# A graph network on one core: the signal of a matmul group stands at a drain of TensorE's queue instead of on its last matmul, in four stages

## The chip, the cores and the metric

One Trainium2 chip, of which the kernel uses one core. The time is device microseconds of one execution. The kernel before was timed in 3 runs: median 5306.26 us, 5303.0 to 5307.47.

## The reference, cut to what matters

6250 nodes with 256 features each, 100000 edges with a source, a destination (edges sorted by destination), three attributes and one of 8 types. Four graph layers one after the other, each on the normalised and rectified nodes and added to them:

```python
h = relu(layernorm(x)); x = x + L0(h, edge_attr, src, dst)        # edge MLP, sum by dst, W2, unit norm
h = relu(layernorm(x)); x = x + L1(h, (src, dst), edge_type)      # x @ W[r] for 8 relations, sum by src
h = relu(layernorm(x)); x = x + L2(h, (src, dst))                 # attention, 8 heads, sum by dst
h = relu(layernorm(x)); x = x + L3(h, (src, dst))                 # normalised sum by src, @ W + b
```

L0 gathers `h[src]` per edge; since its first product is linear up to the bias, the kernel multiplies the nodes first (a table of 6250 x 256, then a gather per edge). L1 likewise needs `h @ W[r]` for all 8 relations: a table of 6250 x 2048. L0's second product is `relu([h, sum] @ W2.T)`, each row divided by its norm.

## The kernel before, in words

The nodes are 49 tiles of 128 rows, the edges 784 columns of 128. The program is a chain of stages; each is a block in which every engine has its own queue and all engines meet at the end. Some stages run many tiles; a `Ring` writes seven tile steps out and repeats them in a loop with the registers of the tile number.

Edges sorted by source are needed too. A record of 8 numbers per edge is written to its place in a list in DRAM by 784 indirect DMAs (`Scatter.run`, L577), one per column of 128 edges, issued by GpSimd. These are spread over the first stages, as work beneath them: `CUTS` (L29) gives each stage its share, counted in rounds of 16 DMAs. GpSimd waits for the DMAs of a half round before it issues the next half of the following round, and a stage can't end before its share has been issued and has landed.

The stages that matter here, in order, with their share of the scatter:

- `list_stage` by source (no scatter yet; the same code as by destination, but with a mask buffer per bucket, so that VectorE runs ahead), `place_stage` (48 DMAs), then the statistics of the nodes (32).
- `table_stage(0)` (64 DMAs): for each tile ScalarE normalises (L2045), TensorE transposes 2 x 128 columns (L2080) and signals `turned`, ScalarE copies (L2050), TensorE multiplies by the weights (L2091) and signals `made`, VectorE adds the bias (L2065), the result goes to DRAM. An fp32 product appears as two matmuls in the trace, so the 256-column product of two halves is four.
- `list_stage` by destination (112 DMAs): 49 times VectorE writes a mask of the edges of one bucket (L404), and TensorE sums it up in two matmuls (L460) and signals `counted`. There are four mask buffers. Then VectorE ranks the counts and the records leave.
- a tile stage and the edge MLP pass (32 and 16 DMAs).
- `sage_update` (160 DMAs), the first update: for each tile TensorE transposes 4 x 128 columns (L2162, `turned`), VectorE copies (L2196), TensorE multiplies (L2168, `made`), ScalarE rectifies and squares (L2143, L2145). After seven tiles VectorE applies the norms and takes the statistics (L2184 to L1912), and only then copies transposes of the next seven.
- `table_stage(1)` (320 DMAs): as layer 0, but 2048 columns, in four blocks of 512 with one `made` each; VectorE copies each block (L2067).

After them come passes over the edges (832, 831, 832 and 586 tiles) in which GpSimd gathers one tile of 128 rows per indirect DMA (L1760, L1591, L675).

TensorE's instructions are issued in the written order: weight load, matmul, and between the groups waits and register arithmetic of the loop. In the kernel before, the last matmul of a group carries the increment of the semaphore (`last.then_inc(...)`).

Of the kernel before, what the change touches and what calls it, by code (L numbers as in the profile page):

```python
# [115 lines left out]
def wait_count(eng, sem, count):  # L116

    if count is not None and not (isinstance(count, int) and count <= 0):
        eng.wait_ge(sem, count)
# [132 lines left out]
def list_stage(nc, c, edges, other=None, first=0, end=0):  # L252
# [10 lines left out]
    with ExitStack() as st:  # L263
# [15 lines left out]
        masked, counted, ranked = sem("masked"), sem("counted"), sem("ranked")  # L279
# [3 lines left out]
        if not by_dst:  # L283
            raw = [sb(f"raw{f}", [TURN, COLS // TURN, P], I32) for f in range(3)]
            real = [r[:, :, :].bitcast(F32) for r in raw]
            turned, kept, key_ready, rest_ready = sem("turned"), sem("kept"), sem("key_ready"), sem("rest_ready")
# [21 lines left out]
        def turned_bank(f, k):  # L308

            return (ps[2 * f + k // 4], k % 4 * TURN + (16 if (f, k // 4) == (2, 1) else 0))  # L310
# [7 lines left out]
        @block.sync  # L318
        def _(sp):
            sp.wait_ge(zeroed, 2)  # L320
            if by_dst:
                load(sp, dst_i, c.dst_in, 1, 0, key_in)
                load(sp, next_i, c.dst_in, 1, 1, rest_in)
            else:
                load_rows(sp, raw[0], c.src_in, key_in)

                full = (sh.NB - 1) * P
                sp.dma_start(c.x[:, 0:sh.NB - 1, :],
                             c.x_in[0:full, :].rearrange("(i p) d -> p i d", p=P)).then_inc(x_in, 16)
                sp.dma_start(c.x[0:sh.LAST, sh.NB - 1, :], c.x_in[full:sh.N, :]).then_inc(x_in, 16)  # L330
                sp.wait_ge(x_in, 32)
            sp.wait_ge(key_in, 48)
            if by_dst:

                sp.wait_ge(recorded, 1)
                sp.dma_start(edges.to.rearrange("(p n) w -> p (n w)", p=P), rec[:, :, :].rearrange("p n w -> p (n w)")).then_inc(written, 16)
                sp.wait_ge(written, 16)
# [103 lines left out]
        @block.tensor  # L441
        def _(pe):
            def turn(f):

                for k in range(COLS // TURN):
                    bank, at = turned_bank(f, k)
                    last = nc.tensor.transpose(bank[:, at:at + TURN], real[f][:, k, :], c.ident[0:TURN, 0:TURN])
                last.then_inc(turned, 1)

            if not by_dst:  # L450
                pe.wait_ge(key_ready, 1)
                turn(0)
            for d in range(NB):
                if not by_dst and d == 8:
                    pe.wait_ge(rest_ready, 2)
                    turn(1)
                    turn(2)
                pe.wait_ge(masked, d + 1)
                for a, z in col_halves:
                    last = nc.tensor.matmul(psT[0:NB, a:z], c.row_of[:, NB - 1 - d:2 * NB - 1 - d], same[:, d % ring, a:z],  # L460
                                            start=(d == 0), stop=(d == NB - 1), skip_group_check=True)
                last.then_inc(counted, 1)
            if by_dst:
                pe.wait_ge(compared, 2)
                nc.tensor.matmul(ps[5][:, 0:1], c.ones[:, :], falls[:, :], start=True, stop=True).then_inc(fallen, 1)
            pe.wait_ge(ranked, 1)
            nc.tensor.matmul(ps[5][0:NB, 8:9], c.before[0:NB, 0:NB], nb[0:NB, 0:1], start=True, stop=True).then_inc(prefixed, 1)
# [807 lines left out]
class Behind:  # L1275
# [16 lines left out]
    def sem(self, name):  # L1292
        return self.nc.alloc_semaphore(f"{name}_behind_{self.nm}")
# [675 lines left out]
def table_stage(nc, c, layer, edges, first, end):  # L1969
# [8 lines left out]
    with ExitStack() as st:  # L1978
# [11 lines left out]
        w_in, hs, turned, hTs, made, outs = [sem(x) for x in ("w_in", "hs", "turned", "hTs", "made", "outs")]  # L1990
# [4 lines left out]
        @block.gpsimd  # L1995
        def _(pool):
            scatter.run(pool)
# [73 lines left out]
        @block.tensor  # L2071
        def _(pe):
            pe.wait_ge(w_in, 16 * {0: 2, 1: NREL}[layer])

            def step(i, u):
                if (t := ring.at(i, u)) is not None:
                    pe.wait_ge(hs, ring.count(t))
                    wait_count(pe, hTs, ring.count(t, 1 if u == 0 else 2))
                    for k in range(2):
                        last = nc.tensor.transpose(psT[u % 2][:, k * P:(k + 1) * P], h[:, u, k * P:(k + 1) * P], c.ident[:, :])  # L2080
                    last.then_inc(turned, 1)
                if (t := ring.at(i, u, 1)) is not None:
                    pe.wait_ge(hTs, ring.count(t))
                    for b, (a, z) in enumerate(blocks):

                        n = NBK * (ring.count(t) - 1) + b
                        back = 4 if NBK * t[1] + b >= 4 else (4 if (NBK * G) % 4 == 0 else (NBK * t[1] + b) + 1)
                        if not (isinstance(n, int) and n - back + 1 <= 0):
                            pe.wait_ge(outs, n - back + 1)
                        for k in range(2):  # L2090
                            last = nc.tensor.matmul(psO[(NBK * t[1] + b) % 4][:, 0:z - a], hT[:, t[1], k * P:(k + 1) * P],  # L2091
                                                    w[:, k, a:z], start=(k == 0), stop=(k == 1))
                        last.then_inc(made, 1)
            ring.run(pe, step, lag=1)


def sage_update(nc, c, edges, first, end):
# [4 lines left out]
    with ExitStack() as st:  # L2102
# [11 lines left out]
        w_in, hns, turned, turned_back, made, rs, sqs, step_, stated = [sem(x) for x in (  # L2114
            "w_in", "hns", "turned", "turned_back", "made", "rs", "sqs", "step_", "stated")]
# [5 lines left out]
        @block.gpsimd  # L2121
        def _(pool):
            scatter.run(pool)
# [29 lines left out]
        @block.tensor  # L2153
        def _(pe):
            pe.wait_ge(w_in, 16)

            def step(i, u):
                if (t := ring.at(i, u)) is not None:
                    pe.wait_ge(hns, ring.count(t))
                    wait_count(pe, turned_back, ring.count(t, 1 if u == 0 else 2))  # L2160
                    for k in range(4):
                        last = nc.tensor.transpose(psT[u % 2][:, k * P:(k + 1) * P], hn[:, u, k * P:(k + 1) * P], c.ident[:, :])  # L2162
                    last.then_inc(turned, 1)
                if (t := ring.at(i, u, 2)) is not None:
                    pe.wait_ge(turned_back, ring.count(t))
                    wait_count(pe, rs, ring.count(t, 1 if t[1] == 0 else 2))
                    for k in range(4):
                        last = nc.tensor.matmul(psO[t[1] % 2][:, 0:D], hnT[:, t[1], k * P:(k + 1) * P], w[:, k, :],  # L2168
                                                start=(k == 0), stop=(k == 3))
                    last.then_inc(made, 1)  # L2170
            ring.run(pe, step, lag=2)

        @block.vector
# [700 lines left out]
```

## Time and profile before

| | kernel before |
|---|---|
| timed, median of 3 | 5306.26 us |
| the profiled execution, first to last instruction | 6597.1 us |
| mean granted clock of TensorE | 0.714 |
| TensorE matmul busy | 3895.4 us (59%) |
| GpSimd busy | 3799.2 us (58%) |
| VectorE busy | 2562.6 us (39%) |
| ScalarE busy | 1792.3 us (27%) |

The profile is of one execution, with every instruction recorded; its span is the 6597.1 us, and a time around that span isn't given. It is a good deal longer than the timed runs, so a duration from it must be set against the timed median with care. Register, branch, semaphore and drain instructions aren't counted as busy. A matmul's end is modelled from its size. "Idle before" is the time an engine stood still, with what ended it; where the engine named had long been done, it was something else.

### The profile page before, as it was taken

The numbers are of one execution on the slowest core, as the hardware profiler recorded it, in microseconds if no ns is written. First come the engines' busy times: TensorE is split into PE (matmuls) and PEld (weight loads), VectorE is DVE, ScalarE is ACT, GpSimd is POOL, SyncE is SP. The second block draws the span as 40 slices with busy tenths as digits, with TensorE's granted clock in tenths as the row PEclk, the third lists the DMA queues.
The fourth block names the chain that finished last, engine by engine and source line by source line (L and its number), as shares of the span: only waits on it lengthen the run. The fifth ranks groups of instructions, "written<-read, shape, count | busy, mean of one in ns | idle before, by whom it ended". The sixth has DMA issues, their size and how long they took to land. (4 is left out here: it accounts for less than half of the span.)

```text
span 6597.1 us, 65618 instructions
## 1 busy us (share of the span) xinstructions
PE 3895.4 (59%) x14913; PEld 2594.0 (39%) x14914; DVE 2562.6 (39%) x8644; ACT 1792.3 (27%) x5648; POOL 3799.2 (58%) x3942
## 2 busy tenths in 40 slices
PE   4232666667641533596455555566777777577777
PEld 2121333333320510242333333355566555455555
DVE  4223444444430300132222222255555555644443
ACT  0111555555530400011000000044444444400000
POOL 3554666666666077402666666666666666277776
PEclk7565666766665765796676666667777777688888
DMA  1011332332310010144433333323333333233332
GB/s 48 20 41 60 88 88 87 89 89 87 88 45 3 0 42 22 59 148 141 124 99 98 98 98 98 96 82 87 87 87 86 87 86 89 77 98 99 99 98 87
DMA packets 277662, 527.83 MB, mean 80 GB/s; under 512 B 80566, under 2 KB 175259, under 8 KB 277049
## 3 DMA queue, kind: packets, MB, share of 16 engines
q0 software_dynamic: 176144, 422.24, 22.5%
q1 hardware_dynamic: 85200, 86.14, 3.9%
q10 hardware_dynamic: 15960, 15.41, 0.7%
q8 instruction: 137, 2.24, 0.1%
q14 instruction: 221, 1.81, 0.1%
HBM read 433.63 MB, written 89.82 MB: 79 GB/s over the span
## 5 line engine op out<-in xcount | busy, mean ns | idle before, releaser
L675 POOL DMA_INDIRECT got_attend_src_dst<-dram_gtab,gather_src x832 | 800.4, 962 | 531.0 <-DVE msg_attend_src_dst L747 320.9
L577 POOL DMA_INDIRECT dram_rec_src<-rec_src x784 | 766.5, 978 | 509.6 <-issue 243.5
L1760 POOL DMA_INDIRECT got_edge_mlp_src_dst<-dram_ptab,gather_src x832 | 786.3, 945 | 463.2 <-DVE pre_edge_mlp_src_dst L1802 252.9
L1591 POOL DMA_INDIRECT got_rgcn<-dram_xtab,gather_of_type x831 | 788.3, 949 | 392.5 <-issue 187.9
L1886 PE MATMUL psS_edge_mlp_src_dst<-msg_edge_mlp_src_dst,hot_edge_mlp_src_dst 128*128 128x256 f32 x1664 | 736.1, 568 | 434.0 <-DVE sage_sums L1783 223.6
L1591 POOL DMA_INDIRECT got_gcn<-dram_htab,gather_rest x586 | 616.5, 1052 | 234.1 <-issue 148.9
L861 PE MATMUL psS_attend_src_dst<-msg_attend_src_dst,hot_attend_src_dst 128*128 128x264 f32 x1664 | 700.8, 513 | 19.5 <-DVE msg_attend_src_dst L747 14.3
L2091 PE MATMUL psO_tab<-w_tab,hT_tab 128*128 128x512 f32 (+1 forms) x980 | 474.4, 633 | 350.1 <-issue 200.5
L1886 PEld LDWEIGHTS psS_edge_mlp_src_dst<-msg_edge_mlp_src_dst,hot_edge_mlp_src_dst 128*128 128x128 f32 x1664 | 388.5, 269 | 589.7 <-issue 338.8
L1682 PE MATMUL psS_rgcn<-got_rgcn,hot_rgcn 128*128 128x257 f32 x1662 | 543.8, 471 | 79.7 <-DMA got_rgcn<-dram_xtab,gather_of_type 55.0
L1783 DVE TENSOR_TENSOR sage_sums<-sage_sums,psS_edge_mlp_src_dst 128x256 f32 x832 | 347.8, 418 | 523.6 <-PE psS_edge_mlp_src_dst L1886 246.1
L884 PE MATMUL psF_attend_src_dst<-ident,hot_attend_src_dst 128*128 128x128 f32 x832 | 314.4, 378 | 356.2 <-ACT hotT_attend_src_dst L832 190.4
L877 PEld LDWEIGHTS psN_attend_src_dst<-node,hotT_attend_src_dst 128*128 128x128 f32 x1664 | 412.5, 253 | 138.1 <-issue 41.4
L1682 PEld LDWEIGHTS psS_rgcn<-got_rgcn,hot_rgcn 128*128 128x128 f32 x1662 | 362.8, 234 | 237.3 <-issue 169.2
L2091 PEld LDWEIGHTS psO_tab<-w_tab,hT_tab 128*128 128x128 f32 x980 | 199.3, 215 | 573.1 <-issue 409.3
L1850 ACT ACTIVATE msg_edge_mlp_src_dst<-pre_edge_mlp_src_dst 128x256 f32<-128x256 f32 x832 | 340.3, 413 | 293.8 <-DVE pre_edge_mlp_src_dst L1802 211.3
L1802 DVE TENSOR_TENSOR pre_edge_mlp_src_dst<-got_edge_mlp_src_dst,psE_edge_mlp_src_dst 128x256 f32<-128x256 f32 x832 | 344.4, 414 | 158.4 <-remote 104.1
L709 DVE TENSOR_TENSOR sums<-sums,psS_attend_src_dst 128x264 f32 x832 | 350.7, 422 | 64.8 <-issue 31.5
L861 PEld LDWEIGHTS psS_attend_src_dst<-msg_attend_src_dst,hot_attend_src_dst 128*128 128x128 f32 x1664 | 361.1, 266 | 37.2 <-DVE msg_attend_src_dst L747 30.7
L1601 DVE TENSOR_SCALAR hot_rgcn<-iota,rel_src 128x128 f32<-128x128 f32 x831 | 216.9, 315 | 390.4 <-remote 180.5
L2067 DVE COPY out_tab<-psO_tab 128x512 f32<-128x512 f32 x196 | 133.7, 690 | 588.4 <-DMA got_edge_mlp_src_dst<-dram_ptab,gather_src 308.9
L1682 PE MATMUL psS_gcn<-got_gcn,hot_gcn 128*128 128x257 f32 x1172 | 322.8, 409 | 64.8 <-issue 30.8
(397 smaller groups left out, 5878.7 us busy)
## 6 DMA issues: line engine op xcount, KB each, us to landing
dram_xtab<-out_tab SPq DMA_DIRECT2D x48, 1024.0 KB
got_edge_mlp_src_dst<-dram_ptab,gather_src POOLq DMA_INDIRECT x832
got_attend_src_dst<-dram_gtab,gather_src POOLq DMA_INDIRECT x832
got_rgcn<-dram_xtab,gather_of_type POOLq DMA_INDIRECT x831
dram_rec_src<-rec_src POOLq DMA_INDIRECT x784
got_gcn<-dram_htab,gather_rest POOLq DMA_INDIRECT x586
dram_gtab<-sums ACTq DMA_DIRECT2D x48, 132.0 KB
x_sb<-x_in SPq DMA_DIRECT2D x1, 6144.0 KB
```

The costliest lines, as they stand in the source:

```text
L577: nc.gpsimd.indirect_dma_start(edges.to, bass.IndirectOffsetOnAxis(edges.rec[:, column, PLACE:PLACE + 1].bitcast(I32), 0), edges.rec[:, co ...
L675: nc.gpsimd.indirect_dma_start(got[:, t % U, 0:w], None, table, bass.IndirectOffsetOnAxis(row_of[:, t:t + 1], 0)).then_inc(row_in[t % U], 16)
L709: nc.vector.tensor_tensor(here, here, psS[t[1] % banks][:, 0:cols], ALU.add).then_inc(added, 1)
L861: nc.tensor.matmul(psS[t[1] % banks][:, 0:cols], hot[:, t[1], :], rows(t), start=True, stop=True).then_inc(sums, 1)
L877: nc.tensor.matmul(psN[t[1] // 2 % 2][:, 2 * HEADS * (t[1] % 2):2 * HEADS * (t[1] % 2 + 1)], hotT[:, t[1] % 4, :], c.node[:, :, :].rearran ...
L1591: nc.gpsimd.indirect_dma_start(got[:, t % U, 0:D], None, table, bass.IndirectOffsetOnAxis(row_of[:, t:t + 1], 0)).then_inc(row_in[t % U], 16)
L1682: nc.tensor.matmul(psS[b % 2][:, 0:D + 1], hot[:, t % U, :], got[:, t % U, 0:D + 1], start=(k == 0), stop=(k == lay.counts[b] - 1), skip_g ...
L1760: nc.gpsimd.indirect_dma_start(got[:, t % U, 0:width], None, table, bass.IndirectOffsetOnAxis(row_of[:, t:t + 1], 0)).then_inc(row_in[t % ...
L1783: nc.vector.tensor_tensor(here, here, psS[t[1] % banks][:, 0:cols], ALU.add).then_inc(added, 1)
L1802: nc.vector.tensor_tensor(pre[:, t[1] % 4, :], got[:, t[1], 0:D], psE[t[1] % 4][:, 0:D], ALU.add).then_inc(pres, 1)
L1886: nc.tensor.matmul(psS[t[1] % banks][:, 0:cols], hot[:, t[1], :], msg[:, t[1] % 8, :], start=True, stop=True).then_inc(sums, 1)
L2091: last = nc.tensor.matmul(psO[(NBK * t[1] + b) % 4][:, 0:z - a], hT[:, t[1], k * P:(k + 1) * P], w[:, k, a:z], start=(k == 0), stop=(k == 1))
```

## The change

In the list stage (by source and by destination: both run the same line), in both table stages and in the first update, the increment no longer stands on the last matmul or transpose of a group. A `drain` of TensorE's queue follows the group and carries it. There are five places in the code; they make 49 signals in each of the two list stages, 49 + 49 in the first table stage, 49 + 196 in the second and 49 + 49 in the update. All other stages keep the increment on the matmul.

```diff
--- before.py
+++ after.py
@@ -459,7 +459,7 @@
                 for a, z in col_halves:
                     last = nc.tensor.matmul(psT[0:NB, a:z], c.row_of[:, NB - 1 - d:2 * NB - 1 - d], same[:, d % ring, a:z],
                                             start=(d == 0), stop=(d == NB - 1), skip_group_check=True)
-                last.then_inc(counted, 1)
+                nc.tensor.drain().then_inc(counted, 1)
             if by_dst:
                 pe.wait_ge(compared, 2)
                 nc.tensor.matmul(ps[5][:, 0:1], c.ones[:, :], falls[:, :], start=True, stop=True).then_inc(fallen, 1)
@@ -2078,7 +2078,7 @@
                     wait_count(pe, hTs, ring.count(t, 1 if u == 0 else 2))
                     for k in range(2):
                         last = nc.tensor.transpose(psT[u % 2][:, k * P:(k + 1) * P], h[:, u, k * P:(k + 1) * P], c.ident[:, :])
-                    last.then_inc(turned, 1)
+                    nc.tensor.drain().then_inc(turned, 1)
                 if (t := ring.at(i, u, 1)) is not None:
                     pe.wait_ge(hTs, ring.count(t))
                     for b, (a, z) in enumerate(blocks):
@@ -2090,7 +2090,7 @@
                         for k in range(2):
                             last = nc.tensor.matmul(psO[(NBK * t[1] + b) % 4][:, 0:z - a], hT[:, t[1], k * P:(k + 1) * P],
                                                     w[:, k, a:z], start=(k == 0), stop=(k == 1))
-                        last.then_inc(made, 1)
+                        nc.tensor.drain().then_inc(made, 1)
             ring.run(pe, step, lag=1)
 
 
@@ -2160,14 +2160,14 @@
                     wait_count(pe, turned_back, ring.count(t, 1 if u == 0 else 2))
                     for k in range(4):
                         last = nc.tensor.transpose(psT[u % 2][:, k * P:(k + 1) * P], hn[:, u, k * P:(k + 1) * P], c.ident[:, :])
-                    last.then_inc(turned, 1)
+                    nc.tensor.drain().then_inc(turned, 1)
                 if (t := ring.at(i, u, 2)) is not None:
                     pe.wait_ge(turned_back, ring.count(t))
                     wait_count(pe, rs, ring.count(t, 1 if t[1] == 0 else 2))
                     for k in range(4):
                         last = nc.tensor.matmul(psO[t[1] % 2][:, 0:D], hnT[:, t[1], k * P:(k + 1) * P], w[:, k, :],
                                                 start=(k == 0), stop=(k == 3))
-                    last.then_inc(made, 1)
+                    nc.tensor.drain().then_inc(made, 1)
             ring.run(pe, step, lag=2)
 
         @block.vector
```

## Rows read from the trace of the kernel before

**Rows 1.** Costliest groups of instructions: line, engine, what, count, busy us, mean ns, idle

```profile
L577 POOL DMA_INDIRECT dram_rec_src<-rec_src x784 | 766.5, 978 | 509.6 <-issue 243.5
...
L1760 POOL DMA_INDIRECT got_edge_mlp_src_dst<-dram_ptab,gather_src x832 | 786.3, 945 | 463.2 <-DVE pre_edge_mlp_src_dst L1802 252.9
```

**Rows 2.** Timeline, first table stage, GpSimd: start us, duration us, line, [idle before]

```profile
227.29 0.96 POOL L577 DMA_INDIRECT dram_rec_src<-rec_src  x1 [0.30 <-issue]
```

**Rows 3.** Windows: start:end length, PE, PEld, DVE, ACT, POOL busy (count), clock, DMA share

```profile
0.00:77.00 77.00, 40.05 (x230) 22.80 (x232) 43.99 (x121) 4.81 (x7) 8.17 (x29) 0.79 0.33 99
...
306.00:372.00 66.00, 47.10 (x230) 38.35 (x230) 19.02 (x43) 32.99 (x75) 4.14 (x5) 0.84 0.24 80
```

**Rows 4.** Timeline, first table stage beneath the scatter

```profile
246.11 0.66 PE L2080 MATMUL psT_tab<-ident,h_tab 128*128 128x128 f32 x2 [4.60 <-issue]
...
246.56 1.91 PE L2091 MATMUL psO_tab<-w_tab,hT_tab 128*128 128x256 f32 x4
...
255.37 0.43 DVE L2065 TENSOR_TENSOR out_tab<-psO_tab,bias_tab 128x256 f32<-128x256 f32 x1 [11.47 <-DMA dram_rec_src<-rec_src]
...
260.21 0.37 ACT L2050 COPY hT_tab<-psT_tab 128x256 f32<-128x256 f32 x1 [13.74 <-remote]
```

**Rows 5.** Tile stage: timeline of two lines, and the queue's drain (duration ns, start us)

```profile
583.99 2.98 PE L1000 MATMUL psX_tiles<-both_of_src,past_of_src 49*128 49x2 f32 x14
...
610.40 1.11 DVE L967 TENSOR_SCALAR place_table<-ps_tiles 1x512 int32<-1x512 f32 x2 [31.91 <-remote]
...
L1009 PEldq DRAIN  x1: 29318/29318/29318, 581.1 to 581.1; - x1
```

**Rows 6.** Windows: list stage, second table twice, first table, one update round

```profile
395.00:511.00 116.00, 19.55 (x46) 3.71 (x46) 9.21 (x23) 0.00 (x0) 88.05 (x92) 0.50 0.03 3
...
2360.00:2710.00 350.00, 106.98 (x126) 35.74 (x126) 19.36 (x28) 6.21 (x14) 264.34 (x265) 0.56 0.09 24
...
329.00:361.00 32.00, 30.44 (x164) 25.38 (x163) 11.44 (x28) 22.95 (x53) 0.00 (x0) 1.00 0.32 111
...
2171.66:2199.00 27.34, 17.78 (x84) 15.12 (x84) 11.11 (x31) 12.17 (x36) 0.00 (x0) 0.81 0.00 0
...
2760.00:3010.00 250.00, 250.00 (x637) 113.36 (x636) 96.41 (x142) 30.89 (x70) 0.00 (x0) 1.00 0.44 151
```

**Rows 7.** Timeline of both table stages: groups back to back, and one after a pause

```profile
357.40 1.03 PE L2091 MATMUL psO_tab<-w_tab,hT_tab 128*128 128x256 f32 x4
...
358.27 0.38 PE L2080 MATMUL psT_tab<-ident,h_tab 128*128 128x128 f32 x2
...
239.95 0.37 ACT L2050 COPY hT_tab<-psT_tab 128x256 f32<-128x256 f32 x1 [2.75 <-PE psT_tab L2080]
...
240.38 1.13 PE L2091 MATMUL psO_tab<-w_tab,hT_tab 128*128 128x256 f32 x4 [1.97 <-ACT hT_tab L2050]
...
2867.02 7.03 PE L2091 MATMUL psO_tab<-w_tab,hT_tab 128*128 128x512 f32 x16
...
2873.89 0.38 PE L2080 MATMUL psT_tab<-ident,h_tab 128*128 128x128 f32 x2
```

**Rows 8.** Table stages' queues (min/median/max ns), and a wait (us, times, longest)

```profile
L1978 POOLq DRAIN  x2: 5280/9464/13649, 307.9 to 2733.2; - x2
...
L1978 SPq DRAIN  x2: 7/7/7, 367.2 to 3050.2; - x2
...
L2089 PEldq ALU_OP  x75: 32/32/42, 246.2 to 2963.5; - x75
...
PE psT_tab L2080 <- DMA w_tab<-wrel_in: 19.2, 1, 19.2
```

**Rows 9.** Timeline, one update round: eight matmuls early and later in it

```profile
2200.72 3.62 PE L2168 MATMUL psO_sage<-w_sage,hnT_sage 128*128 128x256 f32 x8
...
2207.05 1.89 PE L2168 MATMUL psO_sage<-w_sage,hnT_sage 128*128 128x256 f32 x8
```

**Rows 10.** Timeline, list stage by source

```profile
36.76 14.03 PE L460 MATMUL psT_src<-masks,row_of 128*49 128x512 bf16 x82
```

## The prediction, made before the change was run

> **What bounds the kernel now.** I read the page's list of groups first, then the windows of single stages, then the timeline inside them. GpSimd issues one indirect DMA per 128 rows nearly all the time, each busy 0.95 to 0.98 us, and where nothing holds it the next starts 0.30 us after the end of the last: a pace of 1.26 us [rows 1, 2]. There are five such groups: the two of [rows 1] (784 and 832 issues) and three like them with 832, 831 and 586, together 3865. At 1.26 us that is 4870 us. The stretches in which GpSimd issues none are eleven, 12 to 110 us long; two stand in [rows 3]. With 306 to 372 counted as 8 us, for a reason that follows, they make 443 us. The sum is 5313 us. The timed runs have a median of 5306; the profiled execution has a span of 6597 us (what lies around the span isn't shown). So the timed kernel looks like one bound by GpSimd's issue from end to end, and the profiled execution has 1290 us more.
>
> Where those come from: in the stages with the scatter beneath, TensorE's signals arrive late. A matmul group that starts at 246.56 and lasts 1.91 is seen by VectorE at 255.37, a transpose that ends at 246.77 is seen by ScalarE at 260.21 [rows 4]. While that lasts TensorE does 46 matmuls and 46 loads in 116 us of the list stage, and 126 and 126 in 350 us of the second table stage: 1.26 and 1.39 us for each, though one kind of matmul is 272 to 512 columns of bf16 and the other 512 of fp32 [rows 6]. A cost per instruction that ignores the instruction's size looks like the recording of it, not like its work. I take it that the timed runs don't have it; the sum above says the same.
>
> In such undisturbed stages, what ends last? Second table stage: its own work is 20 us until the weights are there [rows 8], 49 tiles of 7.09 us (2867.02 to 2873.89 plus two transposes, 0.22) [rows 7], 20 us for the last stores, which end at 3050.2 [rows 8]: 387 us. The 320 scatters take 404 us, and GpSimd's queue needs up to 14 more to end [rows 8]: 418 us. Update: seven rounds of 27.3 [rows 6] and some 7 us at the ends, 198 us; 160 scatters, 202, with start and end 212 us. First table stage: 163 loads in 32 us are 27 tiles, 1.18 us each [rows 6], 58 for 49 and 9 at the ends, 67 us; 64 scatters with the end, 87 us. So in each the scatter is late last, with a margin of 31, 14 and 20 us.
>
> **The change.** It takes the increment off the last matmul of a group and puts a drain with the increment behind it: 49 in the list stage by destination, 49+49 in the first table stage, 49+196 in the second, 49+49 in the update. The line of the list stage serves the one by source too, which comes first and has no scatter beneath it: 49 more, 539 in all. Nothing else moves.
>
> What a drain costs. The kernel has TensorE drains only at stage ends, so no row shows one between groups; the pieces are in the rows. First, overlap that is lost: four matmuls start at 357.40 and last 1.03 us, yet the next transposes start at 358.27; the same 0.16 us stands between 2867.02 + 7.03 and 2873.89 [rows 7]. Behind a drain the next group can't start before the last has ended. Second, the drain itself: the one of the tile stage ends at 581.1 + 29.3 = 610.4, within 0.1 us of the moment at which VectorE goes on [rows 5]; I take 0.05. Third, the restart: ScalarE's copy ends at 240.32, the matmuls start at 240.38, and the group lasts 1.13 us instead of 1.03 [rows 7]: 0.05 and 0.10. Together 0.36 us. Fourth, what is queued behind the drain: the register instructions and waits of the next group. They now run ahead beneath matmuls; behind a drain they are exposed. There are 3 to 5 per tile, and one is busy 0.03 to 0.05 us [rows 8]; with fetching I take 0.1 each. Bounds for a drain with everything: 0.2 us (overlap and little else) and 0.6. Below nothing is excluded as long as signals come promptly, since the drain waits for the same matmul that signalled before. ScalarE and VectorE get the signal 0.05 us later, and they aren't on the path of TensorE-bound tiles.
>
> The Trainium skill (PSUM — Partial Sum Buffer, "Engine vs sequencer instructions") speaks against this change: the increment belongs on the matmul, a drain is for a separate barrier and waits until the engine is wholly idle. TensorE: Matmul & The Clock Gate ("Part 2: What happens when you issue a matmul") puts the part that one matmul hides under the next at about 166 ns; the 0.16 us of the trace agree, and by the page alone the 539 drains would expose 89 us, against the 194 that 0.36 us give.
>
> Second table stage: 5 x 0.36 + 4.7 x 0.1 = 2.27 us a tile, 111 us for 49. Own work 387 + 111 = 498, against 418: **+80**. Bounds: 5 x 0.2 gives +18, 5 x 0.6 gives +116.
> Update: 2 x 0.36 + 0.31 = 1.03 a tile, 50 us; TensorE is on the path for all seven tiles of a round (17.8 of 27.3 us busy). 198 + 50 = 248 against 212: **+36**; bounds +6 and +45.
> First table stage: 2 x 0.36 + 0.33 = 1.05 a tile, 51 us; 67 + 51 = 118 against 87: **+31**; bounds 0 and +39.
> List stage by source: the last 82 matmuls, 41 groups, run back to back in 14.03 us while nothing else is under way and VectorE waits for their end [rows 10]. 41 x 0.36 = **+15**; bounds +8 and +25. Nothing covers it.
> List stage by destination: 49 x 0.4 = 20 us, under 112 scatters (141 us) of which the stage's own work takes less than half: **0**, and 20 if that cover were gone.
> Sum +162 us: 5306 + 162 = **5468 us**; all lower bounds together +32, all upper +225, or +245 with the list stage by destination uncovered.
>
> **The rivals.**
> The late signals are real in timed runs, and the drain cures them (it goes faster). For it: in the trace they hold up all four stages, together 1452 us (225 to 553 and 1927 to 3051); the changed ones are just those. With drains that signal at once the four would take 498 + 248 + 118 + 150 = 1014 us, 438 less; with the 15 of the list stage by source 423 less, scaled by 5306/6597 340, so 4966 us. It decides from the point where a drain beneath the scatter ends promptly. Against it: the one drain in the trace that meets the scatter. TensorE's last matmul ends at 586.97, and the drain ends at 610.4, 23 us late, after the scatter; VectorE gets the matmul's own signal at the same 610.40 [rows 5]. So the drain waits for what is late. Against it too is the sum of 5313.
> They are real and the drain doesn't cure them: then only tiles after the scatter's end pay, some 37 of 49 in each stage: 84 + 38 + 39 = 161 us, with the 15 of the list stage 176, scaled 142, 5448 us. This lies in the same range.
> A drain costs next to nothing, 0.1 us or less: then the margins of 31, 14 and 20 us swallow it but for the 4 us of the list stage by source, 5306 to 5310 us. The margins speak for it, the 0.16 us of overlap against it.
> The clock falls: in the update's rounds a group of eight 256-column matmuls takes 3.62 us just after TensorE had waited for VectorE and 1.89 us later in the same round [rows 9], so pauses can cost half the speed, at the 1.2 instead of the 2.4 GHz level. If the 0.4 us pauses of the second table stage did that, its 49 x 6.8 us of matmul would double: 333 more, 5801 us. The granted clock was 1.00 in the first table stage's steady stretch at 95% TensorE busy and 0.81 over a round at 65% [rows 6]; after the change the table stages stand near 75% in pauses of less than half a microsecond, not ten as in a round. The Trainium skill (TensorE: Matmul & The Clock Gate, "HAM oscillation") has the clock fall in gaps of some microseconds; by that too it should stay up.
>
> **How the numbers follow.** The forecast, with the second rival, in which drains just cost too: 0.76, its own range 5338 to 5551. Faster by the cure: 0.12. Nearly free: 0.08. The clock falls: 0.04. What a measurement of this kernel can tell from no change is about 0.2%, or 11 us. Faster 0.12, within 0.2% 0.08, slower 0.80. The range 5300 to 5600 leaves out the cure, the fallen clock and a small part of the forecast's tail.
>
> **What would show it.** In the profile after, the steady tile of the second table stage should be 9.4 instead of 7.09 us, that of the first 2.2 instead of 1.18, a round of the update near 34.5 instead of 27.3; signals beneath the scatter should be as late as before, and the 41 groups of the list stage by source 29 us instead of 14; the profiled span should be longer by 130 to 200 us. GpSimd's pace stays at 1.26. I am wrong if the steady tiles grow by less than 1 us in the second table stage, if drains beneath the scatter end within a microsecond of their matmuls, or if the timed kernel is not slower although the tiles are: then the scatter's margin was larger than I have it.

## The result, and the profile after

The changed kernel takes 5493.21 us (median of 4 runs, 5491.73 to 5499.66), the kernel before in the same comparison 5306.86 (5303.0 to 5308.14): a ratio of 1.0352, with a 95% interval from 1.0339 to 1.0365. The change costs 186 us. The forecast was 5468, range 5300 to 5600, slower with a chance of 0.80.

The profiled execution of the changed kernel has a span of 5491.7 us. The rows of before come from an execution of 6597 us, and I had to know whether its 1290 us more belonged to the kernel, so I had the kernel before profiled once more (first experiment): span 5298.6 us. Rows of before in what follows are from that second execution, if nothing else is said. It allows a table by stage, in us, from one meeting of all engines to the next:

| stage | before | after | difference | forecast |
|---|---|---|---|---|
| start and list by source | 55.8 | 67.2 | +11.4 | +15 |
| first table | 88.4 | 169.0 | **+80.6** | +31 |
| list by destination | 167.0 | 167.8 | +0.8 | 0 |
| update | 211.5 | 241.2 | +29.7 | +36 |
| second table | 419.4 | 489.1 | +69.7 | +80 |

Every other stage is within 1.2 us of before. The five sum to +192, the two spans differ by 193. Three terms came out a little smaller than forecast, one as forecast (within 1 us), and one is 2.6 times its forecast.

The page of the changed kernel has GpSimd's groups as they were (beside [rows 1]; count, busy us, mean ns, idle us):

```profile
L1760 POOL DMA_INDIRECT got_edge_mlp_src_dst<-dram_ptab,gather_src x832 | 786.7, 946 | 255.6 <-issue 220.6
L577 POOL DMA_INDIRECT dram_rec_src<-rec_src x784 | 765.8, 977 | 316.6 <-issue 242.4
```

977 ns each, and 0.30 us between them in the stages' timelines: the pace of [rows 1, 2]. So GpSimd issues as before and then waits at the end of the changed stages. The windows of the stage ahead of the first table stage and of the three stages, after (start:end, length, busy us of PE, PEld, DVE, ACT, POOL, granted clock, DMA share, GB/s):

```profile
153.00:198.00 45.00, 0.00 (x0) 0.00 (x0) 23.12 (x108) 1.53 (x2) 30.63 (x32) 0.50 0.03 3
198.00:367.00 169.00, 132.55 (x294) 71.64 (x294) 20.82 (x49) 43.40 (x98) 61.29 (x64) 0.51 0.14 42
1680.00:1921.00 241.00, 143.09 (x588) 101.25 (x588) 79.00 (x220) 85.06 (x253) 155.53 (x160) 0.83 0.03 5
1921.00:2410.00 489.00, 409.84 (x882) 143.27 (x882) 135.04 (x196) 43.40 (x98) 306.38 (x320) 0.97 0.36 112
```

and before, in its second profiled execution:

```profile
187.00:275.00 88.00, 58.03 (x294) 47.77 (x294) 20.78 (x49) 43.41 (x98) 61.26 (x64) 0.83 0.26 81
1587.00:1799.00 212.00, 123.46 (x588) 105.01 (x588) 78.99 (x220) 85.05 (x253) 154.81 (x160) 0.78 0.04 6
1799.00:2218.00 419.00, 349.24 (x882) 158.15 (x882) 133.63 (x196) 43.40 (x98) 306.44 (x320) 0.92 0.42 131
```

GpSimd's 64, 160 and 320 issues take the same time in both, within 1 us. In the first table stage the same 294 matmuls are busy 132.6 us instead of 58.0, and the granted clock is 0.51 instead of 0.83: TensorE runs at 1.2 GHz until its last group of matmuls. In the other two the clock is no lower than before.

A steady tile of the second table stage after the change, by TensorE's timeline (start, duration, count; it answers to the 16 matmuls in 7.03 us of [rows 7]):

```profile
2261.41 0.41 PE L2080 MATMUL psT_tab<-ident,h_tab 128*128 128x128 f32 x2 [0.32 <-issue]
2262.04 1.98 PE L2091 MATMUL psO_tab<-w_tab,hT_tab 128*128 128x512 f32 x4 [0.22 <-DVE out_tab L2067]
2264.23 1.98 PE L2091 MATMUL psO_tab<-w_tab,hT_tab 128*128 128x512 f32 x4 [0.21 <-issue]
2266.42 4.04 PE L2091 MATMUL psO_tab<-w_tab,hT_tab 128*128 128x512 f32 x8 [0.21 <-issue]
2270.81 0.41 PE L2080 MATMUL psT_tab<-ident,h_tab 128*128 128x128 f32 x2 [0.35 <-issue]
```

From transposes to transposes 9.40 us (median of the stage 9.37; forecast 9.4), before 7.09. The row of eight matmuls is two groups, the third and the fourth block of the tile. Four of the five groups of a tile have a pause of 0.21 to 0.35 us ahead of them; the fourth block has one of 0.08. A group of four lasts 1.98, where four matmuls of the unbroken row lasted 1.88. So a block starts 2.19 us after the one before it (the fourth 2.06), against 1.72 before.

The trace holds the drains too. In this tile each ends 0.02 us after the end of its group's last matmul. Ahead of the fourth block no register instruction stands in TensorE's queue, and its first matmul starts 0.06 us after the drain's end; ahead of the second and third one register instruction does, and it is 0.19 us.

The first table stage after the change:

```profile
231.52 0.66 PE L2080 MATMUL psT_tab<-ident,h_tab 128*128 128x128 f32 x2 [0.32 <-issue]
232.41 2.04 PE L2091 MATMUL psO_tab<-w_tab,hT_tab 128*128 128x256 f32 x4 [0.23 <-issue]
234.77 0.66 PE L2080 MATMUL psT_tab<-ident,h_tab 128*128 128x128 f32 x2 [0.32 <-issue]
```

A tile is 3.25 us: 0.66 and 2.04 of matmul, 0.55 of pauses. In [rows 6] it was 1.18, and four of these matmuls took 1.03 [rows 7]. (A tile here is counted from transposes to transposes.)

The queues at the end of the table stages, after (min/median/max ns, first and last start in us); GpSimd's is empty long before SyncE's ends:

```profile
L1978 POOLq DRAIN  x2: 5280/6636/7991, 281.0 to 2333.1; - x2
...
L1978 SPq DRAIN  x2: 7/7/7, 366.8 to 2409.6; - x2
```

and before, the other way round:

```profile
L1978 SPq DRAIN  x2: 7/7/7, 256.1 to 2178.3; - x2
...
L1978 POOLq DRAIN  x2: 5280/6636/7991, 269.7 to 2209.8; - x2
```

The last indirect DMA is issued 88 us before the end of the first table stage, 35 before that of the update and 80 before that of the second table stage (8, 7 and 11 before the change). In all three another engine now ends last.

### The profile page after: what moved, and what is told of

It reads as the page before. It is cut to its first block and busy times, and to the rows that moved or that the text cites. A ratio compares the mean times of both kernels' runs of the same rounds, so it can differ in the third digit from the quotient of the medians.

```text
span 5491.7 us, 66153 instructions
## 1 busy us (share of the span) xinstructions
PE 3990.7 (73%) x14909; PEld 2371.6 (43%) x14914; DVE 2600.0 (47%) x8644; ACT 1794.2 (33%) x5648; POOL 3802.8 (69%) x3942
## 5 line engine op out<-in xcount | busy, mean ns | idle before, releaser
L1682 PE MATMUL psS_rgcn<-got_rgcn,hot_rgcn 128*128 128x257 f32 x1662 | 746.4, 552 | 242.0 <-DMA got_rgcn<-dram_xtab,gather_of_type 201.7
L1886 PE MATMUL psS_edge_mlp_src_dst<-msg_edge_mlp_src_dst,hot_edge_mlp_src_dst 128*128 128x256 f32 x1664 | 686.5, 535 | 230.3 <-DVE sage_sums L1783 159.1
L861 PE MATMUL psS_attend_src_dst<-msg_attend_src_dst,hot_attend_src_dst 128*128 128x264 f32 x1664 | 615.1, 456 | 79.3 <-DVE msg_attend_src_dst L747 70.8
L1886 PEld LDWEIGHTS psS_edge_mlp_src_dst<-msg_edge_mlp_src_dst,hot_edge_mlp_src_dst 128*128 128x128 f32 x1664 | 366.4, 255 | 371.1 <-ACT msg_edge_mlp_src_dst L1850 290.9
L1682 PE MATMUL psS_gcn<-got_gcn,hot_gcn 128*128 128x257 f32 x1172 | 366.3, 419 | 196.8 <-DMA got_gcn<-dram_htab,gather_rest 128.8
L877 PEld LDWEIGHTS psN_attend_src_dst<-node,hotT_attend_src_dst 128*128 128x128 f32 x1664 | 336.8, 216 | 172.7 <-issue 114.8
L884 PE MATMUL psF_attend_src_dst<-ident,hot_attend_src_dst 128*128 128x128 f32 x832 | 282.5, 340 | 100.9 <-ACT hot_attend_src_dst L817 96.5
L747 DVE TENSOR_TENSOR msg_attend_src_dst<-got_attend_src_dst,msg_attend_src_dst 128x256 f32<-128x256 f32 x832 | 347.5, 418 | 0.7 <-issue 0.7
L861 PEld LDWEIGHTS psS_attend_src_dst<-msg_attend_src_dst,hot_attend_src_dst 128*128 128x128 f32 x1664 | 298.0, 222 | 114.8 <-DVE msg_attend_src_dst L747 111.2
L1682 PEld LDWEIGHTS psS_gcn<-got_gcn,hot_gcn 128*128 128x128 f32 x1172 | 197.8, 195 | 321.9 <-DVE hot_gcn L1601 174.4
```

Of the source, the lines that this page charges most:

```text
L747: nc.vector.tensor_tensor(msg[:, t[1] % 8, 0:D].rearrange("p (h d) -> p h d", d=DH), got[:, t[1], 0:D].rearrange("p (h d) -> p h d", d=DH) ...
L861: nc.tensor.matmul(psS[t[1] % banks][:, 0:cols], hot[:, t[1], :], rows(t), start=True, stop=True).then_inc(sums, 1)
L1682: nc.tensor.matmul(psS[b % 2][:, 0:D + 1], hot[:, t % U, :], got[:, t % U, 0:D + 1], start=(k == 0), stop=(k == lay.counts[b] - 1), skip_g ...
L1886: nc.tensor.matmul(psS[t[1] % banks][:, 0:cols], hot[:, t[1], :], msg[:, t[1] % 8, :], start=True, stop=True).then_inc(sums, 1)
```

## The experiments

All are edits of the kernel before. Line numbers and the kernel's names are those of the profile.

**The kernel before, profiled once more.** No edit.

> The kernel before, profiled a second time. Theory: the late signals of TensorE belong to the first profiled execution and not to the timed ones; the timed kernel paces itself by GpSimd's issue at 1.26 us per DMA. Then this profile, if it is not stretched, has a span near 5305 us, the second table stage lasts 415 to 440 us (320 scatters and the queue's end), the update 205 to 215, the first table stage 85 to 95, the list stage by destination 145 to 170, and a block of the first table stage is seen by VectorE within 0.1 us of its end. If it is stretched again (span near 6600 us), recording this kernel stretches it, and the timed runs (5306 us) don't have that. Rival: the late signals are in the timed runs too; then an unstretched profile can't exist, and the span is 6600 us with the same late signals.

Measured: 5300.28 us, span 5298.6, clock 0.798, and the stages as long as the theory said (the table above). In the first table stage, beneath the scatter, a product that ends at 230.86 is seen by VectorE at 230.89:

```profile
229.83 1.03 PE L2091 MATMUL psO_tab<-w_tab,hT_tab 128*128 128x256 f32 x4
...
230.89 0.42 DVE L2065 TENSOR_TENSOR out_tab<-psO_tab,bias_tab 128x256 f32<-128x256 f32 x1 [0.66 <-PE psO_tab L2091]
```

So the 1290 us and TensorE's late signals of [rows 4] belong to that one profiled execution; what made them is not shown. The sum of 5313 us, GpSimd's issue from end to end, describes the timed kernel, though its closeness is partly luck. The last gathers are slower than 1.26 us, 1.36 each with the idle time before them,

```profile
L1591 POOL DMA_INDIRECT got_gcn<-dram_htab,gather_rest x586 | 617.5, 1054 | 178.4 <-issue 102.2 <-PE psS_gcn L1682 76.1
```

some 57 us that the sum doesn't have, and the stretches without issues are shorter by about as much.

**Each part of the change by itself.** Each has the change in one stage (the two list stages count as one) and leaves the matmul's own signal in the others. In the table stages (only the product's line is shown, for the first stage; the signal of the transposes is changed likewise, and for the second stage it says `layer == 1`):

```diff
-                        last.then_inc(made, 1)
+                        (nc.tensor.drain() if layer == 0 else last).then_inc(made, 1)
```

> Drains in the two list stages alone, 98 of the 539. Theory: only the stage by source pays, since nothing runs beneath it: the changed kernel's profile shows 0.589 us a group there against 0.34 before, for 41 groups 10 us; the stage by destination is covered by the scatter. 5317 us, 5312 to 5322 (+0.2%). Rival: the stage by destination pays too (it lasted 168 us in the changed kernel where 112 scatters take 141): 5330 to 5340 us.

> Drains in the first table stage alone, 98 of the 539. Theory: the pauses keep TensorE's granted clock at the lower level there (0.50 to 0.52 in the changed kernel's profile, 1.00 in the steady stretch of before), so that a tile takes 3.25 us instead of 1.18; the stage lasts 169 us against 87 to 90: 5306 + 80 = 5386 us, 5375 to 5395, granted clock of the stage near 0.5. Rival, as I predicted it: the clock stays up and a drain costs 0.36 us, 1.05 us a tile: 5337 us.

> Drains in the second table stage alone, 245 of the 539. Theory: 0.36 us a drain and the exposed register instructions, 2.3 us a tile, the clock near 1.0; the stage lasts 489 us against 418: 5377 us, 5365 to 5390. Rival: the stage's margin beneath the scatter is larger (the stage before lasts 435 us or more because the scatter lands late): 5355 us or less.

> Drains in the first update alone. Theory (the parts of the change add up, each delaying only its own stage): the stage goes from 211.5 us to 241, and the time is 5307 + 30 = 5337 us; what the other three parts left of the 186 us is 28. Rival (part of this stage's growth belongs to the clock or the order that the drains of the stages before it leave behind): less than 20 us alone, under 5327 us.

| drains in | us | ratio, 95% interval | us more than before |
|---|---|---|---|
| list stages | 5318.48 | 1.0028 [1.0017, 1.004] | 12.8 |
| first table | 5383.24 | 1.0147 [1.013, 1.0164] | 77.6 |
| second table | 5374.06 | 1.013 [1.0113, 1.0146] | 68.4 |
| update | 5336.59 | 1.0058 [1.0041, 1.0075] | 29.5 |

All four lie where the theory had them. The sum is 188.3 us, the whole change 186.4: the parts add up, and in each profile its own stage is the one that grew. (The runs with drains in the list stages scatter more than the others, from 5311.86 to 5331.88; in the profile that stage is 12 us longer.) With drains in the first table stage alone that stage takes 169.2 us at a clock of 0.51, so its slow clock comes from its own drains and not from a stage before it. The update is at 0.84, in the same rhythm as in the whole change.

In the list stage by source the 41 back-to-back groups of [rows 10] (14.03 us) are one row again, after and before (second execution):

```profile
37.09 24.25 PE L460 MATMUL psT_src<-masks,row_of 128*49 128x512 bf16 x82
```

```profile
35.90 14.10 PE L460 MATMUL psT_src<-masks,row_of 128*49 128x512 bf16 x82
```

10.15 us for 41 drains: 0.25 us each (0.27 and 0.29 in the profiles of the run with drains in the list stages alone and of the next one, where the 41 groups took 25.02 and 26.06 us).

**The drain without the signal.** (One of the five places is shown.) In all five the signal stays on the last matmul, and a drain that signals nothing follows it.

```diff
                         last.then_inc(made, 1)
+                        nc.tensor.drain()
```

> The signals stay on the last matmul of each group, as in the kernel before, and a drain that signals nothing stands behind it in all five places. Theory (what costs is that TensorE's queue stands at the drain until the group is through, so that the next matmul starts late, and where TensorE then shows 1.2 GHz; who sends the signal does not matter): the time of the change, 5490 us, with the first table stage near 169 us and the second near 489. Rival (what costs is that the signal leaves later): the time of the kernel before, 5306 us.

Measured: 5499.98 us, ratio 1.0366 [1.0347, 1.0385], the changed kernel's time within the intervals (1.0352 [1.0339, 1.0365]). Its first table stage:

```profile
198.00:367.00 169.00, 132.81 (x294) 71.62 (x294) 20.79 (x49) 43.43 (x98) 61.28 (x64) 0.50 0.13 42
```

Who sends the signal doesn't matter. The price is that of the drain in TensorE's queue.

**A second drain beside the first.** In the second table stage, with the one stage's drains:

```diff
+                        if layer == 1:
+                            nc.tensor.drain()
+                        (nc.tensor.drain() if layer == 1 else last).then_inc(made, 1)
```

> Drains in the second table stage alone, as in the run that had only these (5374 us), and a second, bare drain ahead of each of its four drains for the product: 196 drains more, each of which finds TensorE already empty or is followed at once by one that does. Theory (a drain's price is the lost overlap of the matmuls around it, paid once, and the queue's own handling is small): 0.05 to 0.1 us each, 10 to 20 us, so 5384 to 5394 us. Rival (each drain costs its 0.35 us whatever stands before it): 196 x 0.35 = 69 us, 5443 us.

Measured: 5390.74 us, ratio 1.0154 [1.0137, 1.0171]: 16.7 us more than with one drain, 0.085 us for each of the 196. The median tile grows from 9.37 to 9.72 us. The pause ahead of a group grows by this:

```profile
2107.76 1.98 PE L2091 MATMUL psO_tab<-w_tab,hT_tab 128*128 128x512 f32 x4 [0.29 <-issue]
2110.04 1.98 PE L2091 MATMUL psO_tab<-w_tab,hT_tab 128*128 128x512 f32 x4 [0.29 <-issue]
```

0.29 instead of 0.21 (and 0.16 instead of 0.08 ahead of the fourth block). A group lasts 1.98 either way. So of the 0.46 us that one drain of this stage costs (2.28 a tile / 5), some 0.08 is the queue's handling of a drain; the rest is paid once, for standing between two groups of matmuls.

**One drain a tile in the first table stage.** Only the product's signal, and then only the transposes'.

```diff
-                        last.then_inc(made, 1)
+                        (nc.tensor.drain() if layer == 0 else last).then_inc(made, 1)
```

> The drain only at the signal of the product in the first table stage, one per tile in place of two; everything else as before. The stage took 88 us before and 169 with both drains, where the granted clock stood at 0.51. If the clock stays at its upper level with one drain, a tile costs 1.18 + 0.4 = 1.6 us, the stage 88 + 49 x 0.1 to 0.4 = 92 to 108 us, and the time is 5310 to 5325 us. If it falls here too, a tile takes about 2.7 us (3.25 less one drain's 0.5), the stage some 140 us, and the time is 5355 us.

```diff
-                    last.then_inc(turned, 1)
+                    (nc.tensor.drain() if layer == 0 else last).then_inc(turned, 1)
```

> The drain only at the signal of the transposes in the first table stage, one per tile; the one of the product is left out. With the product's drain alone the stage took 93.5 us at a granted clock of 0.95, with both 169 at 0.50. Theory (it is the number of pauses, or the two together, that brings the clock down): the clock stays up here too, a tile takes 1.6 to 1.7 us, the stage 92 to 96 us, and the time is 5311 to 5315 us. Rival (it is this drain, with two short matmuls between two pauses, that brings the clock down): a tile takes about 2.7 us, the stage 140 us, and the time is 5355 us.

Measured: 5310.56 us, ratio 1.0005 [0.9996, 1.0015], and 5305.64, ratio 0.9999 [0.999, 1.0009]. The stage takes 93.5 and 88.9 us (88.4 before). The second is less than its theory had (92 to 96 us, 5311 to 5315): the scatter's margin swallowed nearly all of it. The windows of the stage, product's drain only:

```profile
187.00:198.00 11.00, 5.89 (x16) 3.75 (x17) 0.85 (x2) 4.08 (x9) 7.12 (x8) 0.50 0.18 50
198.00:276.00 78.00, 62.14 (x280) 40.92 (x278) 19.51 (x46) 39.32 (x89) 54.17 (x57) 0.98 0.26 81
```

Transposes' drain only:

```profile
187.00:198.00 11.00, 6.29 (x16) 3.84 (x16) 0.67 (x2) 4.09 (x9) 7.31 (x8) 0.50 0.18 50
198.00:270.00 72.00, 60.09 (x273) 43.60 (x273) 19.30 (x46) 39.34 (x89) 53.97 (x57) 1.00 0.28 86
```

With either alone the clock rises within some 15 us of the stage's first matmul and stays, and the mean tile is 1.71 and 1.61 us instead of 1.22: 49 x 0.4 to 0.5, 20 to 24 us, about the margin that the scatter leaves. So 49 drains cost nothing here that the timed runs can tell, and the other 49 some 75 us: their own pauses, which nothing covers any more, and the clock, which with both stays low. Neither place is guilty by itself.

**More matmuls in the first table stage.** Both drains, and each product computed twice into the same place.

```diff
-                        for k in range(2):
+                        for k in (0, 1, 0, 1) if layer == 0 else range(2):
```

> Both drains in the first table stage, and each tile's product of four matmuls computed twice into the same place, so the output is the same and TensorE has 1.71 us (at 2.4 GHz 0.86) more of matmuls in each tile. If it is the low share of matmuls between the pauses that holds the clock at its lower level, the clock rises to the upper one, and a tile takes at most 1.63 of work at the lower level halved plus the pauses, about 3.1 us: the stage is 160 us or less in spite of more work, and the time 5376 or less. If the clock stays low, a tile takes 3.25 + 1.71 = 4.96 us, the stage 252 us, and the time is 5468 us.

Measured: 5373.32 us, ratio 1.0121 [1.0104, 1.0138]: 196 more matmul instructions, and 10 us less than without them (66 more than the kernel before beside it, instead of 78). The stage takes 155.5 us instead of 169.2. Two tiles of it, and its windows:

```profile
241.12 0.41 PE L2080 MATMUL psT_tab<-ident,h_tab 128*128 128x128 f32 x2 [0.35 <-issue]
241.76 1.97 PE L2091 MATMUL psO_tab<-w_tab,hT_tab 128*128 128x256 f32 x8 [0.23 <-issue]
...
244.05 0.41 PE L2080 MATMUL psT_tab<-ident,h_tab 128*128 128x128 f32 x2 [0.32 <-issue]
```

```profile
187.00:198.00 11.00, 6.22 (x16) 3.76 (x17) 0.42 (x1) 3.65 (x9) 7.45 (x8) 0.52 0.14 38
198.00:336.00 138.00, 111.06 (x469) 76.60 (x467) 19.63 (x47) 39.76 (x90) 53.83 (x57) 1.00 0.15 47
```

A tile is 2.93 us with eight product matmuls at 2.4 GHz, 3.25 with four at 1.2. (The 3.1 us of the expectation doesn't come out of its terms: the matmuls of a tile, 0.66 + 2.04 + 1.71 us at the lower level, halved, and 0.55 of pauses make 2.76.)

**A burst once.** This run tells whether the pauses bring the clock down or keep it from rising. The windows of before show that the stage begins at the lower level and that the clock rises at once:

```profile
186.00:192.00 6.00, 1.05 (x4) 0.72 (x4) 0.00 (x0) 1.91 (x5) 3.22 (x4) 0.50 0.27 67
192.00:198.00 6.00, 5.96 (x20) 4.75 (x20) 0.95 (x3) 3.04 (x8) 4.48 (x6) 0.58 0.14 41
198.00:204.00 6.00, 5.54 (x32) 4.54 (x31) 2.05 (x6) 4.47 (x10) 4.75 (x5) 1.00 0.38 120
```

and after the change it doesn't:

```profile
198.00:204.00 6.00, 1.84 (x5) 1.05 (x6) 0.00 (x0) 2.83 (x7) 3.83 (x4) 0.50 0.24 68
204.00:210.00 6.00, 5.38 (x13) 2.84 (x13) 0.85 (x2) 1.66 (x5) 4.57 (x5) 0.50 0.10 25
210.00:240.00 30.00, 25.12 (x57) 13.70 (x57) 3.82 (x9) 8.54 (x19) 22.68 (x25) 0.50 0.17 48
...
360.00:366.00 6.00, 1.88 (x5) 1.17 (x4) 0.85 (x2) 0.00 (x0) 0.00 (x0) 0.78 0.12 38
```

It stays at 0.50 for 160 us and rises only in the stage's last microseconds (the last row), where the last two products follow each other without transposes between them, 0.23 us apart.

Both drains as in the run with only this stage, and the product of the first of its 49 tiles ten times over (its output is unchanged):

```diff
-                        for k in range(2):
+                        first = layer == 0 and t[1] == 0 and isinstance(t[0], int) and t[0] == 0
+                        for k in (0, 1) * (10 if first else 1):
```

> Both drains in the first table stage, and the product of the first of its 49 tiles computed ten times over into the same place, some 12 us of matmuls without a pause; the other 48 tiles have both drains and nothing more, as in the run that took 5383 us with the stage at 169. In that run the granted clock is 0.50 when the stage begins and 0.50 in all 27 stretches of 6 us after it; in the kernel before it rises to 1.00 within the first 12 us of tiles. Theory (the pauses don't bring the clock down, they keep it from rising in a stage that begins at the lower level): once the burst has raised it, it stays up, a tile takes 2.93 us (product twice, clock 1.00) less the 0.86 of the second product, 2.07, the stage 9 + 12 + 48 x 2.07 = 120 us, and the time is 5307 + 32 = 5339 us. Rival (with this share of matmuls the clock falls back wherever it starts): a tile takes 3.25 us again, the stage 181 us, and the time is 5395 us.

Measured: 5342.16 us beside 5313.65 of the kernel before, ratio 1.0052 [1.0035, 1.0069]. The theory said +32, the rival +88; it is +28.5. The burst, and a tile 37 us after it:

```profile
193.42 11.52 PE L2092 MATMUL psO_tab<-w_tab,hT_tab 128*128 128x256 f32 x40
...
242.32 0.41 PE L2080 MATMUL psT_tab<-ident,h_tab 128*128 128x128 f32 x2 [0.35 <-issue]
...
242.96 1.10 PE L2092 MATMUL psO_tab<-w_tab,hT_tab 128*128 128x256 f32 x4 [0.23 <-issue]
```

```profile
187.00:198.00 11.00, 5.96 (x15) 4.28 (x16) 0.00 (x0) 3.22 (x7) 6.82 (x8) 0.50 0.14 38
198.00:204.00 6.00, 6.00 (x28) 5.20 (x27) 0.00 (x0) 0.00 (x0) 4.69 (x5) 0.94 0.03 3
204.00:210.00 6.00, 5.07 (x22) 3.05 (x21) 1.27 (x3) 2.42 (x6) 4.56 (x5) 1.00 0.16 47
210.00:240.00 30.00, 21.67 (x87) 12.36 (x85) 5.97 (x15) 12.77 (x29) 22.69 (x25) 1.00 0.23 70
```

The 36 extra matmuls take some 9.5 us (11.52 for forty, where four at the lower level take 2.04), and the stage is 121.3 us long instead of 169.2. The timed run is 41 us shorter, or 49 when each is taken against the kernel before beside it. The same pauses, 0.55 us in a median tile of 2.06, don't bring the clock down once it is up: it reads 1.00 in each 30-us window to 300. So with the same code in 48 of its 49 tiles the stage ran at either level nearly to its end, and what TensorE did in the first tile picked the level. A burst later in the stage was not tried.

No run points to a version that beats both kernels: GpSimd's issue bounds the kernel before, and nothing here touches it.

## Why the prediction was right, and which term was mis-sized

- **What bounds the kernel** (GpSimd's issue; the timed runs don't have the late signals): right. The second execution of before spans 5298.6 us against the sum of 5313, in which a pace that is too fast for the last gathers and stretches that are too long nearly cancel. The cure rival (4966) had nothing to cure.
- **The price of a drain** (0.36 us and 0.1 for each exposed register instruction): right, in sum and in its parts. Ahead of the fourth block, with no register instruction behind the drain, it is 2.06 - 1.72 = 0.34 us: 0.16 of lost overlap, 0.02 until the drain's end, 0.06 until the next matmul, and a group longer by 0.10 (the forecast had 0.16, 0.05, 0.05 and 0.10). One register instruction adds 0.13. Second table stage, five drains a tile: 9.37 - 7.09 = 2.28, forecast 2.27. First table stage at the upper clock level, two a tile: 2.06 - 1.08 = 0.98 by the medians, forecast 1.05. Update: 3.14 us from tile to tile within a round instead of 2.17, 0.97, forecast 1.03. In the list stage, with matmuls of bf16 and no register instruction behind the drain, it is 0.25 to 0.29, forecast 0.36; why it is less was not looked into. "Nearly free" is refuted.
- **That the drain and not the place of the signal costs**: shown by the bare drains. I had assumed it.
- **Margins of the scatter** (forecast 31, 14, 20 us for second table stage, update and first table stage): measured 40, 17 and 19. In the second table stage of before, SyncE's last drain (2178.3) puts the stage's own work at 380 us, where I had 387; with 111 more that is 491, measured 489. This is most of the 10 us that its +80 was too much. In the update VectorE's last drain (1781.8) puts it at 195 where I had 198. The margin of some 20 in the first table stage is what hides a single drain a tile.
- **List stage by destination 0**: right, +0.8.
- **First table stage +31: the term that was mis-sized.** The price of the drains was right, the clock was not. At 1.2 GHz a tile has 2.70 us of matmul instead of 1.51; (2.70 - 1.51) x 49 = 58 us. The kernel before also spends its first tiles there, and its own work ended 19 us ahead of the scatter (SyncE's last drain of the stage at 256.1, the end at 275.3): 69 + 48 for the pauses (49 x 0.98) - 88.4 is +29, the rest of the 80.6, some 52, is the clock. The burst run gives nearly the same: 121.3 less the 9.5 of extra matmuls is 112, +23 with the clock up. I had the mechanism among the rivals, priced for the second table stage alone (5801, chance 0.04) and argued from the steady clock of 1.00 in the first [rows 6] that short pauses wouldn't bring it down. That is so: the burst shows it. What I didn't ask is at which level the stage starts. TensorE does nothing in the stage before it (153 to 198 us, 0 matmuls, clock 0.50), so it starts at 0.50; the clock need not fall to cost time, it is enough that it doesn't rise. The second table stage starts at 0.50 too, but with sixteen matmuls of 512 columns to a tile it rises: 0.56 in the window 1930 to 1936 us of the changed kernel and 1.00 from 1936 on.
- The Trainium skill bears on this in a place that I had not weighed: TensorE: Matmul & The Clock Gate ("A second HAM failure mode: psum-queue depth-cycling") tells of short idle spells between matmul groups that make the clock go up and down. The trace agrees that pauses under a microsecond can matter to the clock, but not in the form: in no stretch of the stage does it go up and down; without the burst it stays at 0.50 until the stage's last group, with it at 1.00 from 204 us to the last group.
- **The profile's tests.** The tiles were as said, except the first table's (3.25 instead of 2.2), and the update's rounds take 34 us (forecast 34.5). That signals beneath the scatter would be as late as before was wrong, and "drains that end within a microsecond of their matmuls" was no sign against the forecast: both rested on the belief that every recording of this kernel has the late signals. The profiled span is 193 us longer than that of the second execution of before (forecast 130 to 200).

That the total came out within 25 us is partly luck, because the errors have opposite signs: +50 for the first table stage, -10, -6 and -4 for the others, and -6 for what the stages show beyond the timed runs.

Open: what it takes in a stage's first microseconds for the clock to rise was not measured, nor why a drain costs less in the list stage.

## What to carry to other kernels

A drain behind a TensorE group costs 0.25 to 0.49 us of TensorE time here whoever sends the signal, so leave the increment on the last matmul, and count a stage's drains against the margin of what else ends it: in the first table stage 49 were free, 98 cost 78 us. When a change puts pauses into a TensorE stage, look at the granted clock at the stage's start as well as in its steady part: a stage that begins at 1.2 GHz may stay there to its last group, and then all its matmuls are slow. Before explaining a profile that is much longer than the timed runs, take a second one.

## What I had not expected of the hardware

- Adding work made the kernel faster: with both drains in the first table stage 5383.24 us, with 196 matmul instructions more 5373.32, with one burst of 11.5 us 5342.16 (the kernel before beside them: 5305.68, 5307.23 and 5313.65).
- A drain right beside another costs 0.085 us, though the first costs 0.25 or more; the price of the first is the next group's late start, and 0.13 us more for a register instruction behind it.
- One profiled execution of the kernel before took 6597 us, with TensorE's signals up to 23 us late beneath the indirect DMAs [rows 4, 5]; the twelve later profiles of it, the changed kernel and the variants are not stretched (spans 5298.6 to 5491.7 us).
